# First expert product with stationary weights: the tokens stream, bias and gelu in one ScalarE operation

## The reference

```
logits = xf @ Wg + bg
idx = jnp.argmax(gates, axis=-1)
h = jax.nn.gelu(jnp.einsum('th,ehi->tei', xf, W1) + b1, approximate=False)
y = jnp.einsum('tei,eih->teh', h, W2) + b2
out = jnp.take_along_axis(y, idx[:, None, None], axis=1)[:, 0, :]
```

## Time and profile before

| | |
|---|---|
| median of 3 runs | 511.59 us (509.14 to 511.91) |
| span of the profiled execution, first to last instruction | 495.3 us |
| own full time of the profiled execution | not given; the median is 16.3 us above the span |
| TensorE busy | 436.0 us, 88% |
| VectorE, ScalarE, GpSimd busy | 52%, 41%, 38% |
| chain of work that ended last | 81% TensorE; L1254 alone 28%, L1258 14% |

### The profile page before, as it was taken

How to read it: one execution, slowest core, us unless ns; L and a number is a source line. 1 busy time by engine, 2 the same in 40 slices (tenths; PEclk the granted TensorE clock), 3 DMA queues, 4 the chain that set the end, 5 groups by cost and what they waited for, 6 DMA issues and landing times.

```text
span 495.3 us, 9245 instructions
## 1 busy us (share of the span) xinstructions
PE 436.0 (88%) x2362; PEld 257.4 (52%) x2363; DVE 258.2 (52%) x604; ACT 200.7 (41%) x411; POOL 189.8 (38%) x274
## 2 busy tenths in 40 slices
PE   6758999997999999920699999999999999999991
PEld 2355565565777676610355555555555555555540
DVE  0246999674577677767244444444444444434440
ACT  1142366547788887652122222222222222222220
POOL 7000002300054545453245545545545545545530
PEclk9969999999999999975799999999999999999996
DMA  8999985905356555684522222322222222222200
GB/s 254 309 314 384 376 280 209 369 2 207 121 155 203 166 174 171 180 328 145 183 79 88 71 78 81 88 81 79 91 71 85 85 84 85 70 85 74 65 2 0
DMA packets 33850, 73.97 MB, mean 149 GB/s; under 512 B 4376, under 2 KB 4388, under 8 KB 33575
## 3 DMA queue, kind: packets, MB, share of 16 engines
q1 hardware_dynamic: 26591, 54.22, 34.5%
q0 software_dynamic: 6400, 19.23, 10.2%
q10 hardware_dynamic: 840, 0.29, 0.4%
HBM read 54.50 MB, written 21.06 MB: 153 GB/s over the span
## 4 chain that ended last, share of the span: by engine, by line
PE 81%; DMA 5%; DVE 3%; issue 3%; POOL 2%; SPq 1%; ACT 1%; POOLq 0%; DVEq 0%; ACTq 0%
PE bank L1254 28%; PE bank L1258 14%; PE bank L1198 5%; PE bank L1180 5%; DMA work<-in_ctx 5%; PE bank L1160 4%; PE bank L1110 4%; PE bank L1270 3%; PE bank L1246 3%; PE bank L1088 3%; PE bank L1173 3%; PE bank L1191 1%; PE bank L1070 1%; PE bank L1183 1%; PE bank L1139 1%
## 5 line engine op out<-in xcount | busy, mean ns | idle before, releaser
L1254 PE MATMUL bank<-expert_weights,work 128*128 x624 | 149.2, 382 | 7.5 <-issue 5.8
L1254 PEld LDWEIGHTS bank<-expert_weights,work 128*128 128x128 f16 x624 | 61.3, 98 | 66.2 <-issue 11.3
L1258 PE MATMUL bank<-expert_weights,work 128*128 x312 | 80.5, 381 | 0.0
L696 ACT ACTIVATE work<-bank 128x512 f16<-128x512 f32 x39 | 23.3, 597 | 102.6 <-PE bank L1246 102.6
L981 DVE SCALAR_TENSOR_TENSOR work<-bank,keys_then_b 128x512 f32<-128x512 f32 x39 | 27.0, 692 | 64.1 <-PE bank L1258 64.1
L571 ACT ACTIVATE expert_weights<-expert_weights 128x512 f16<-128x512 f32 (+1 forms) x64 | 38.7, 626 | 40.2 <-DVE expert_weights L774 39.4
L997 DVE SCALAR_TENSOR_TENSOR work<-bank,work 128x512 f32<-128x512 f32 x39 | 27.0, 692 | 52.9 <-PE bank L1258 52.9
L707 ACT ACTIVATE work<-bank 128x512 f16<-128x512 f32 x39 | 23.3, 597 | 69.7 <-PE bank L1270 69.7
L521 POOL DMA_INDIRECT out_x<-work,output_ids x39 | 40.1, 1028 | 26.5 <-DVE work L997 18.7
L1258 PEld LDWEIGHTS bank<-expert_weights,work 128*128 128x128 f16 x312 | 30.7, 98 | 37.5 <-issue 1.1
L516 POOL TENSOR_TENSOR work<-work,values_then_b 128x512 f32<-128x512 f32 x39 | 49.1, 1258 | 0.0
(11 more groups left out here) (154 smaller groups left out, 613.6 us busy)
## 6 DMA issues: line engine op xcount, KB each, us to landing
expert_weights<-in_L_ffn_W SPq DMA_DIRECT2D x14, 1024.0 KB, 9.3
work<-routed_rows SPq DMA_DIRECT2D x39, 258.0 KB, 2.7
expert_weights<-in_x SPq DMA_DIRECT2D x16, 512.0 KB, 8.7
expert_weights<-in_x SPq DMA_DIRECT2D x32, 256.0 KB, 3.0
routed_rows<-values_then_b POOLq DMA_DIRECT2D x9, 258.0 KB, 9.3
expert_weights<-in_L_ffn_W SPq DMA_DIRECT2D x8, 256.0 KB, 3.1
keys_then_b<-in_L_ffn_b SPq DMA_DIRECT2D x1, 2048.0 KB, 7.8
values_then_b<-in_L_ffn_b SPq DMA_DIRECT2D x1, 2048.0 KB, 10.5
```

The lines of the kernel that those rows point to most:

```text
L1254: mm(o, a[:, 0, c, :], w_split[:, bass.ds(first + (2 * c + h) * D, D)], start=(c == 0 and h == 0), stop=False)
L1258: last = mm(o, a[:, 1, c, :], w_split[:, bass.ds(first + 2 * c * D, D)], start=False, stop=(c == C - 1))
```

## The change

- The first product has the expert's weights stationary and the 128 tokens moving: for each of four chunks k of the hidden columns 12 matmuls of 128 columns, so 48, in place of 12 of 512. The result has the hidden columns on the partitions, so it is the transpose of what it was.
- b1 is now one number for each partition. It is loaded with the small biases (32 more rows of `bias_rows`, transposed into `bias_columns`), and the broadcast table is gone. ScalarE adds it in the gelu's own operation, four of 128 columns, with the bias's column given by a register; for this ScalarE reads a value from the table for each tile. VectorE's `bias` is gone.
- The gelu comes out as the second product needs it: `transpose_g` is gone, and `gT_high` and `gT_low` read the gelu from SBUF.
- `up` waits for the low part of `x2T` at its start; on VectorE `finish` is moved behind `gT_low`.

```diff
-            def gelu(j):
-                act.wait_ge(hb_done, j + 1)
-                act.wait_ge(tg_done, j)
-                nc.scalar.activation(gel, hid, ACT.Gelu).then_inc(g_done, 1)
+            def gelu(j):
+                ex = act.value_load(table[0:1, 3, bass.ds(j, 1)], min_val=0, max_val=(E - 1) * C)
+                act.wait_ge(h_done, j + 1)
+                act.wait_ge(gl_done, j)
+                for k in range(C):
+                    nc.scalar.activation(gel[:, P * k:P * (k + 1)], bank[1][:, P * k:P * (k + 1)], ACT.Gelu,
+                                         bias=bcol[:, bass.ds(ex + NB + k, 1)], scale=1.0 / WSCALE).then_inc(g_done, 1)
...
             def gT_high(j):
-                act.wait_ge(tg_done, j + 1)
+                act.wait_ge(g_done, C * j + C)
                 act.wait_ge(y_done, j)
-                nc.scalar.activation(gelT[:, 0, :, :], bank[2][:, :].rearrange("p (c t) -> p c t", c=C),
-                                     ACT.Copy).then_inc(gh_done, 1)
+                nc.scalar.activation(gelT[:, 0, :, :], gel.rearrange("p (c t) -> p c t", c=C), ACT.Copy).then_inc(gh_done, 1)
...
             def step(j, r):
-                if not isinstance(j, int) or j + 1 < NJ:
-                    bias(j + 1)
                 if not isinstance(j, int) or j + 2 < NJ:
                     x2T_low(j + 2)
-                finish(j, r)
                 if not isinstance(j, int) or j + 1 < NJ:
                     gT_low(j + 1)
+                finish(j, r)
...
             def up(j, ex):
-                pe.wait_ge(x2h_done, j + 1)
-                pe.wait_ge(hb_done, j)
-                product(bank[1][:, :], x2T, ex, x2l_done, j).then_inc(h_done, 1)
-
-            def transpose_g(j):
...
+                pe.wait_ge(x2l_done, j + 1)
+                pe.wait_ge(g_done, C * j)
+                for k in range(C):
+                    for c in range(C):
+                        for u, v in PARTS:
+                            last = mm(bank[1][:, P * k:P * (k + 1)], w_split[:, bass.ds(ex + (2 * c + u) * D + P * k, P)],
+                                      x2T[:, v, c, :], start=(c == 0 and u + v == 0), stop=(c == C - 1 and u == 1))
+                last.then_inc(h_done, 1)
...
             def step(j, ex, ex_before):
                 up(j, ex)
                 transpose_x2(j + 1)
                 down(j - 1, ex_before)
-                transpose_g(j)
```

More of the change, by code:

```diff
@@ L154, in build @@
         eota = sb("expert_numbers", [P, E])
-        table = sb("tile_table", [P, 3, NJ], I32)
+        table = sb("tile_table", [P, 4, NJ], I32)
         rows = work[:, 0:U * ROW].rearrange("p (u r) -> p u r", u=U)
@@ L192, in build @@
         res = [carve(D) for _ in range(R)]
-        xn2, x2T, hid, gel, gelT = (carve(D) for _ in range(5))
+        xn2, x2T, gel, gelT = (carve(D) for _ in range(4))
         ge = carve(NJ * E).rearrange("p (j e) -> p j e", j=NJ)
@@ L963, in _ @@
                                            ALU.add).then_inc(tabled, 1)
[L965 removed]
+            for n, width in ((1, NW * 2 * D), (2, D), (3, C)):
                 nc.vector.tensor_scalar(table[:, n, :], tv[:, 0, :], float(E - 1), float(width), ALU.min,
                                         ALU.mult).then_inc(tabled, 1)
[L968 removed]
+            dve.wait_ge(tabled, 4)
             for n in range(n_low, E * NW):
                 low(n)
[L973 removed]
             for u in range(U):
                 dve.wait_ge(sent[u], 16 * NTURN)
[L977 to L982 removed]
             def x2T_low(j):
@@ L1247, in transpose_x2 @@
                 last.then_inc(tx2_done, 1)
-            def product(o, a, first, low_ready, j):
-                for c in range(C):
-                    for h in range(2):
-                        mm(o, a[:, 0, c, :], w_split[:, bass.ds(first + (2 * c + h) * D, D)],
-                           start=(c == 0 and h == 0), stop=False)
-                pe.wait_ge(low_ready, j + 1)
-                for c in range(C):
-                    last = mm(o, a[:, 1, c, :], w_split[:, bass.ds(first + 2 * c * D, D)], start=False, stop=(c == C - 1))
-                return last
-            def up(j, ex):
-                pe.wait_ge(x2h_done, j + 1)
-                pe.wait_ge(hb_done, j)
-                product(bank[1][:, :], x2T, ex, x2l_done, j).then_inc(h_done, 1)
-            def transpose_g(j):
-                pe.wait_ge(g_done, j + 1)
-                pe.wait_ge(gl_done, j)
-                for c in range(C):
-                    last = nc.tensor.transpose(bank[2][:, P * c:P * (c + 1)], gel[:, P * c:P * (c + 1)], ident[:, :])
-                last.then_inc(tg_done, 1)
+            def up(j, ex):
+                pe.wait_ge(x2l_done, j + 1)
[6 more added lines that the diff above has]
+                last.then_inc(h_done, 1)
             def down(j, ex):
@@ L1275, in down @@
                 pe.wait_ge(out_done, j)
-                product(bank[3][:, :], gelT, ex + C * 2 * D, gl_done, j).then_inc(y_done, 1)
+                first = ex + C * 2 * D
+                for c in range(C):
+                    for h in range(2):
+                        mm(bank[3][:, :], gelT[:, 0, c, :], w_split[:, bass.ds(first + (2 * c + h) * D, D)],
+                           start=(c == 0 and h == 0), stop=False)
+                pe.wait_ge(gl_done, j + 1)
+                for c in range(C):
+                    last = mm(bank[3][:, :], gelT[:, 1, c, :], w_split[:, bass.ds(first + 2 * c * D, D)],
+                              start=False, stop=(c == C - 1))
+                last.then_inc(y_done, 1)
             def experts(j, n):
```

37 lines of the change are left out of this document (14 added, 23 removed).

## The result

The changed kernel takes 551.57 us (549.91 to 553.36, four runs) beside 511.75 us (509.14 to 513.35, four runs) of the kernel before: ratio 1.0799, interval 1.0756 to 1.0841, so +39.8 us; 547 was forecast. Its profiled execution took 549.98 us with a span of 548.3.

The account below looks back on a forecast made before the run. TensorE's array was taken to bound the loop before, its sequencer's issue after a gelu wait afterwards: 31 x 0.97 + 5 x 0.89 + 1.3 - 0.2 = +35.6 us, span 530.9, plus 16.3 outside it, 547 us; range 535 to 560.

Parts of the forecast that it names:

- The array's work: TensorE's array in the tile loop: 5.73 us needed per tile, 0.32 less than before, with 0.056 us a pair.
- The sequencer's pace: TensorE's issue of the first product: 32 register operations at 0.131 us each, so at least 4.06 us.
- The chain from s to the first pair: Transposes, copy, value load and four gelus before the next first product: first pair at s + 2.96, period 7.02 us.
- Turns: Each of five turns of the six-tile loop: period 7.96 us, +0.89.
- Start and end: Outside the loop's periods: +1.3 us up to tile 2's transposes, -0.2 us from tile 38's transposes to the last matmul.
- 12.6: Time in us from tile 38's transposes to the last matmul after the change, 12.8 before.
- The sum: All terms of the expert stage together: +35.6 us, span 530.9, time 547 us.
- TensorE's clock: In the loop it should stay full although the array idles 1.3 us in each tile; called open.
- instruction blocks: Rival: longer loop body reloads them at turns; four unhidden give 577 us, one stall 555; 0.09 shared with slower pairs.
- The sequencer's pace isn't hidden by running ahead: First product's issue waits for the previous tile's gelu, so nothing is issued ahead; array idles 1.3 us a tile.
- The array-bound case: Rival, chance 0.06: register operations cost less, the array's 5.73 us a tile bind, -12 us, 500 us.
- the value load doesn't delay the gelu: Rival, chance 0.08: ScalarE's gelu starts at s + 1.3, period 6.7 us, 536 us.

Follow-up runs that it names:

- fixed_dve: Changed kernel with the first product's weights at a constant place (no expert choice) and row normalisation moved from GpSimd to VectorE: 484.65 us, ratio 0.9672.
- xhat_dve: Changed kernel with only the row normalisation moved from GpSimd to VectorE: 539.52 us, ratio 1.0788 to the kernel before.
- load_ahead: Changed kernel with ScalarE's value load for the gelu moved ahead of the copy of the next tile's rows: 541.25 us, ratio 1.0535.
- before_again: The kernel before, unchanged, profiled once more: 519.89 us, span 518.2.
- ahead: Changed kernel with two PSUM banks, value load ahead, normalisation on VectorE, x2T in two buffers and transposes one tile further ahead: 500.9 us, ratio 1.0022.
- fixed_weights: Changed kernel with the first product's weights always expert 0's, at a constant place, so without its register operations: 525.47 us, ratio 1.0245.
- twelve: Kernel of ahead with TensorE's experts loaded in pieces over the turn, and twelve tiles in a loop turn instead of six: 523.14 us, ratio 1.0202.

## Why the prediction was right, and where its numbers were off

**The array's work: right.** 5.73 us a tile was forecast; fixed_dve, where the array idles 0.9 us in the whole loop, has 5.71. A pair costs 0.056 us (2.84 us for 48). The Trainium skill ("TensorE: Matmul & The Clock Gate", Back-to-back issue gap) has some 81 ns for such a pair; these runs don't show it: 48 pairs at 0.081 would take 3.9 us. In the changed kernel a pair does take 0.079 to 0.085, near that number, but for the register operations' sake, as xhat_dve and fixed_dve show.

**The sequencer's pace: right, slightly too dear.** 0.131 us a register operation was taken, 0.127 measured; 4.06 us from first to last pair forecast, 3.95 measured (409.7 to 413.6).

**The chain from s to the first pair: the mis-sized term.** s is the start of the last pair of the first product, 406.35 or so (402.60 + 3.97 - 0.23). "Behind it comes the value load [...]: 0.7 us" took VectorE's 313 ns as the price of the load itself. On ScalarE it is 274 to 562 ns, median 440, over 35 tiles, and 557 in the tile shown. The copy starts at s + 0.97 for 0.81, the gelu 1.07 behind it for 0.8, so at s + 2.04 for 1.6, and the first pair at s + 3.3 for 2.96. The shorter issue (3.95 for 4.06) gives back what the late copy costs, so that where the load is short (288) the period is 7.0, as forecast; where it is long, 7.3. Over the loop, the 14 ordinary periods with a load of at most 310 ns take 6.99 to 7.19 us, the 8 with 547 or more 7.27 to 7.30. The mean of the 31 ordinary periods is 7.16, +1.11 us for +0.97: 31 x 0.14 = 4.3 us, nearly the whole error in the loop. load_ahead shows the load on the path: with the load out of it most periods are 6.69.

**Turns: right.** 7.96 forecast, 7.92 to 8.04 measured, +0.88 us for +0.89.

**Start and end.** +1.1 for +1.3 at the start, which is luck: two executions of the unchanged kernel differ by 3.0 us there. At the end +2.3 for -0.2, a wait put at nothing: "12.6" added up matmuls and overlooked that `finish` now stands behind `gT_low`, and that behind this the last second product waits for both. TensorE idles 2.30 us there, 0.77 at the same place before. In the changed kernel:

```profile
531.44 1.03 PE L1256 MATMUL bank<-expert_weights,work 128*128 x4
...
533.23 0.69 DVE L981 TENSOR_TENSOR work<-work 128x512 f16<-128x512 f32 x1 [5.49 <-ACT work L705]
533.84 0.68 DVE L987 SCALAR_TENSOR_TENSOR work<-bank,work 128x512 f32<-128x512 f32 x1
534.77 1.90 PE L1252 MATMUL bank<-expert_weights,work 128*128 x8 [2.30 <-DVE work L987]
```

**The sum.** 34.5 + 1.3 - 0.2 = 35.6 forecast; 38.7 + 1.1 + 2.3 = 42.1 between the two profiled executions, 39.8 between the medians. The spans themselves differ by 53.0 (548.3 and 495.3), of which 10.9 lie ahead of the expert stage (its start at 246.39 and 235.52): this needn't be the change's, for before_again, without any edit, has 254.01.

**What was open.** TensorE's clock stayed full in the loop (1.00 from 260 to 520 us). No instruction blocks come at the turns once the body has run through: four blocks move in the loop, the last at 296 us, before the first turn, and none more until 524. "The sequencer's pace isn't hidden by running ahead": ahead shows that this was the right question, for with the waits gone it is hidden, inside a turn.

**The rivals.** The array-bound case needed a pitch under 0.100; it was 0.127, and fixed_dve shows what it would have given, a ratio of 0.967. That the value load doesn't delay the gelu (6.7, 536 us) is refuted as a forecast and confirmed as a price: load_ahead is that case, 6.69.

## What to carry to other kernels

Before an operand with a run-time address becomes the one that is loaded most often, count its address operations: each costs TensorE's sequencer 0.127 us, whether 128 or 512 columns follow (the medians of both products), and 128 columns cover only 0.056. Then ask whether the sequencer can run ahead of the array at that place; a wait at the head of a product takes that away. "TensorE 99 per cent busy" doesn't say that the array is the bound: compare the busy time of a group with its columns.

And ask of each engine off the path how long its own round is, before you count on a gain: GpSimd's, 6.1 and 7.1 us by turns in fixed_weights, together with its overlap with VectorE's work, took more than half of what the missing register operations should have given (the loop 236.57 us with it, 207.95 without).

## What the runs showed of the hardware

GpSimd and VectorE disturb each other when both work in SBUF. GpSimd's normalisation (L508 before, L502 after) took the same time for every tile in the loop before and not after; VectorE's subtraction of the gelu, which now reads both operands from SBUF, varies too. Before, then the changed kernel, each in its loop (ns, least, median, most):

```profile
L508 POOL TENSOR_SCALAR work<-work x34: 757/758/762, 265.0 to 469.3; 128x512 f32<-128x512 f32 x34
L991 DVE TENSOR_TENSOR work<-bank,work x35: 691/692/693, 265.2 to 476.1; 128x512 f16<-128x512 f32 x35
```

```profile
L502 POOL TENSOR_SCALAR work<-work x30: 760/1206/1302, 261.6 to 475.8; 128x512 f32<-128x512 f32 x30
L981 DVE TENSOR_TENSOR work<-work x30: 691/702/1062, 264.8 to 475.8; 128x512 f16<-128x512 f32 x30
```

The trace of fixed_weights separates the two cases within one execution: of the 36 normalisations from tile 2 on, the 19 that meet no `gT_low` (L981) take 760 to 772 ns, the 17 that overlap one take 1201 to 1206. In the kernel before, 30 of 36 overlap the subtraction that reads the gelu from PSUM, and they take 757 to 762. So what lengthens the normalisation is the overlap with the subtraction that has both operands in SBUF. No run changes that alone.

TensorE's granted clock fell in twelve after the 4.3 us of idleness at a turn. The sums from 333 to 338 and from 338 to 345 us (the clock is the third number from the end):

```profile
333.00:338.00 5.00, 0.79 (x4) 0.18 (x2) 2.34 (x4) 0.63 (x1) 0.17 (x2) 1.00 0.26 96
338.00:345.00 7.00, 6.90 (x62) 5.70 (x63) 1.24 (x2) 1.63 (x5) 3.60 (x5) 0.76 0.24 78
```

It is at 0.5, the level of 1.2 GHz, from 338.0 to 341.5 us, and again behind the next turn from 420.0 to 423.4. In the changed kernel, whose array by the estimate of 48 x 0.056 has 2.7 us of work in each 3.95 us of a first product, it stayed at 1.00 from 260 to 520 us.
